# A graph network kernel: four accumulator banks in the adjacency stage, row groups released before the fourth scatter of the next, 125-row transfers in two parts

## The reference

```
row = concat(src, loops); col = concat(dst, loops)
deg = segment_sum(ones, col); dinv = rsqrt(deg); w = dinv[row] * dinv[col]
h = x
5 times: h = 0.2 * segment_sum(w * h[row], col) + 0.8 * x
x = layernorm(x + h)

gate = silu(edge_attr @ W1.T + b1) @ W2.T + b2 + sum(emb[z[src]] * (emb[z[dst]] @ adaptW.T))
cw   = where(dist < 6, 0.5 * (cos(pi * dist / 6) + 1), 0)
msg  = gate * x[dst] * cw * mult[dst]
agg  = segment_sum(msg, src) / segment_sum(mult[dst], src)
x = layernorm(x + layernorm_gamma_beta(x + agg))
```

## Time and profile before

| | us |
|---|---|
| median of 3 runs | 4159.2 |
| lowest and highest | 4145.71, 4161.85 |
| the profiled execution | 4189.48 |
| its span, first to last instruction | 4187.5 |
| mean granted TensorE clock in it | 0.763 |

### The profile page before, as it was taken

One profiled execution on the slowest core, in us unless ns is written; L12 is line 12 of the kernel. 1 busy time (PEld: TensorE's weight loads), 2 busy tenths in 40 slices (PEclk: granted clock), 3 DMA queues, 4 the chain that ended last, 5 costly groups with the idle time before them and its releaser, 6 DMA issues. The chain is left out here.

```text
span 4187.5 us, 105568 instructions
## 1 busy us (share of the span) xinstructions
PE 2724.7 (65%) x35364; PEld 2317.5 (55%) x35364; DVE 2724.8 (65%) x5976; ACT 1370.5 (33%) x4059; POOL 2366.0 (57%) x2008
## 2 busy tenths in 40 slices
PE   0455555555656457777877777877737777777773
PEld 0344343344434246667766766766737777677673
DVE  3876676677667454544554454554478888888887
ACT  0443333333334211111110111111136666666662
POOL 1266776777667635555555555655545555555552
PEclk9975555555555578888998888988968788888886
DMA  4543343333342277777878778877646666666663
GB/s 178 185 154 125 124 157 121 139 139 140 139 127 90 84 267 285 285 280 283 294 277 296 273 270 299 293 274 288 234 163 225 213 222 215 214 219 214 218 221 96
DMA packets 228041, 871.37 MB, mean 208 GB/s; under 512 B 89156, under 2 KB 148420, under 8 KB 182787
## 3 DMA queue, kind: packets, MB, share of 16 engines
q1 hardware_dynamic: 166914, 728.89, 48.8%
q10 hardware_dynamic: 9696, 96.89, 5.8%
q0 software_dynamic: 51232, 42.56, 3.4%
HBM read 670.80 MB, written 197.52 MB: 207 GB/s over the span
## 5 line engine op out<-in xcount | busy, mean ns | idle before, releaser
L705 POOL DMA_INDIRECT slot_table<-w_pay,w_slot x1568 | 1773.3, 1131 | 1166.2 <-PEq L1217 509.6
L1219 PE MATMUL pL<-p_parts,p_adj 128*128 128x144 bf16 x12250 | 978.9, 242 | 350.8 <-issue 241.3
L1219 PEld LDWEIGHTS pL<-p_parts,p_adj 128*128 128x128 bf16 x12250 | 891.5, 106 | 433.2 <-issue 429.3
L1031 PE MATMUL pA<-ohk,ohb 128*128 128x98 bf16 x3200 | 359.1, 275 | 550.3 <-ACT adj L1067 370.1
L1031 PEld LDWEIGHTS pA<-ohk,ohb 128*128 128x128 bf16 x3200 | 257.5, 131 | 680.8 <-ACT adj L1067 430.4
L1587 ACT ACTIVATE h_all<-c_rows,c_ac 128x48 f32<-128x48 f32 x2401 | 561.1, 323 | 66.6 <-DVE c_ac L1556 66.6
L1067 ACT ACTIVATE adj<-pA 128x392 bf16<-128x392 f32 x800 | 368.5, 494 | 539.5 <-remote 297.1
L1463 POOL TENSOR_TENSOR c_msg<-c_msg 128x637 f32<-128x637 f32 x196 | 232.8, 1188 | 481.1 <-DVE c_msg L1525 481.1
L792 ACT ACTIVATE w_hid<-w_pH,b1c 96x512 f32<-96x512 f32 x196 | 133.7, 682 | 919.7 <-PE w_pH L740 487.9
L1662 PE MATMUL cG<-c_tabp,c_ohT 128*128 128x81 bf16 x7056 | 369.6, 222 | 4.2 <-DVE c_msg L1525 2.6
L1662 PEld LDWEIGHTS cG<-c_tabp,c_ohT 128*128 128x128 bf16 x7056 | 346.1, 112 | 5.2 <-DVE c_msg L1525 3.1
(11 more groups left out here) (277 smaller groups left out, 3266.5 us busy)
## 6 DMA issues: line engine op xcount, KB each, us to landing
p_adj<-adj_table SPq DMA_DIRECT2D x250, 1568.0 KB
c_lanes<-lane_table SPq DMA_DIRECT2D x150, 768.0 KB, 6.7
adj_table<-adj ACTq DMA_DIRECT2D x50, 1568.0 KB
c_rows<-slot_table SPq DMA_DIRECT2D x255, 255.0 KB, 3.9
slot_table<-zero SPq DMA_DIRECT2D x42, 1249.5 KB
c_lanes<-lane_table SPq DMA_DIRECT2D x50, 832.0 KB
w_attr<-in_edge_attr_dram SPq DMA_DIRECT2D x49, 640.0 KB
slot_table<-w_pay,w_slot POOLq DMA_INDIRECT x1568
```

The lines of the kernel that those rows point to most:

```text
L705: pool.indirect_dma_start(slotT, bass.IndirectOffsetOnAxis(ap=slot[:, t:t + 1], axis=0), pay[:, t, :], None, bounds_check=SLOTS - 1, oob_i ...
L1031: m = nc.tensor.matmul(pA[:, n % 2, j * KG:(j + 1) * KG], ohb[:, b % OB, g * (PT // 2) + j, :], ohk[:, b % OB, g * (PT // 2) + j, :])
L1219: x_ = nc.tensor.matmul(pL[:, half, o * H3:(o + 1) * H3], adj[:, q, n * P:(n + 1) * P], parts[:, n, :, :].rearrange("p t f -> p (t f)"), s ...
```

## The change

Three edits.

Transfers of 124 or 125 rows are split at row 112 (`SPW`): the loads of `dst`, `src` and `ew`, the eight stores of `key_sb` and the store of `cw`. The counts that are waited for follow.

`pA` has four banks for two. PSUM has room for it because `pR` is gone: `labels` write into the unused end of bank 1 of `w_pG`, `offsets` into that of bank 0, and `pC` has a bank of its own in the index stage. In the adjacency stage the gates of chunk 0, which write bank 0, also wait until `off_b` has been copied; in the propagate stage the flag `offsets_first` is False and they don't.

In `scatter`, the wait for the landing of the chunk before and the count of `s_free` stand before the fourth scatter of a chunk, for after its eighth.

```
+    SPW = 112
...
-                pC, pZ, pQ = win.pR, win.pG, win.pT
+                pC = ps("pC", [P, 512], c=c)
+                pZ, pQ = win.pG, win.pT
...
-                            sp.dma_start(shifted[n, 0:E].rearrange("(p j) -> p j", p=SP_), key_sb[:, n * AL:n * AL + ST]).then_inc(s_edge, 16)
+                            to = shifted[n, 0:E].rearrange("(p j) -> p j", p=SP_)
+                            sp.dma_start(to[0:SPW, :], key_sb[0:SPW, n * AL:n * AL + ST]).then_inc(s_edge, 16)
+                            sp.dma_start(to[SPW:SP_, :], key_sb[SPW:SP_, n * AL:n * AL + ST]).then_inc(s_edge, 16)
...
-                        pool.wait_ge(s_edge, 16 * (SH + 1))
+                        pool.wait_ge(s_edge, 16 * (2 * SH + 1))
...
-            pR = ps("w_pR", [P, 512], c=c)
+            GATES = CT // 2 * 2 * H
+            assert GATES + P <= 512 and GATES + NB <= 512
+            offs = pG[:, 0, GATES:GATES + NB]
+            labs = pG[:, 1, GATES:GATES + P]
...
                     for t in range(a, b):
+                        if t == a + 3:
+                            v = (q - 1) % MC
+                            n = 16 * (chunks[v][1] - chunks[v][0])
+                            pool.wait_ge(s_sc[v], w * n + n)
+                            pool.sem_inc(s_free, 1)
                         if before_each:
                             before_each(t)
...
-                    v = (q - 1) % MC
-                    n = 16 * (chunks[v][1] - chunks[v][0])
-                    pool.wait_ge(s_sc[v], w * n + n)
-                    pool.sem_inc(s_free, 1)
...
-            def gates(pe, w, q):
+            def gates(pe, w, q, offsets_first):
...
+                if q == 0 and offsets_first:
+                    pe.wait_ge(s_offb, w + 1)
...
-                nc.tensor.matmul(pR[:, P:2 * P], ones_w[:, :], diag[:, :]).then_inc(s_lab, 1)
+                nc.tensor.matmul(labs, ones_w[:, :], diag[:, :]).then_inc(s_lab, 1)
...
-                nc.tensor.matmul(pR[:, 0:NB], before[:, :], tot[:, :]).then_inc(s_off, 1)
+                nc.tensor.matmul(offs, before[:, :], tot[:, :]).then_inc(s_off, 1)
...
-                nc.scalar.activation(off_b[:, :], pR[:, 0:NB], ACT.Copy).then_inc(s_offb, 1)
+                nc.scalar.activation(off_b[:, :], offs, ACT.Copy).then_inc(s_offb, 1)
...
-                pA = ps("pA", [P, 2, 512], c=c)
+                BANKS = 4
+                pA = ps("pA", [P, BANKS, 512], c=c)
...
-                                    m = nc.tensor.matmul(pA[:, n % 2, j * KG:(j + 1) * KG], ohb[:, b % OB, g * (PT // 2) + j, :],
+                                    m = nc.tensor.matmul(pA[:, n % BANKS, j * KG:(j + 1) * KG], ohb[:, b % OB, g * (PT // 2) + j, :],
...
-                        act.sem_inc(s_ev, 2)
+                        act.sem_inc(s_ev, BANKS)
...
-                                        act.dma_start(tile[0:SP_ - 1, :], bass.AP(table.tensor, 0, [[ST, SP_ - 1], [1, ST + HALO]])).then_inc(s, 16)
+                                        for a, b in ((0, SPW), (SPW, SP_ - 1)):
+                                            act.dma_start(tile[a:b, :], bass.AP(table.tensor, a * ST, [[ST, b - a], [1, ST + HALO]])).then_inc(s, 16)
...
-                                    act.dma_start(ew[:, :], edge_weight.rearrange("(p j) -> p j", p=SP_)).then_inc(s_edges[2], 16)
+                                    for a, b in ((0, SPW), (SPW, SP_)):
+                                        act.dma_start(ew[a:b, :], edge_weight.rearrange("(p j) -> p j", p=SP_)[a:b, :]).then_inc(s_edges[2], 16)
```

More of the change, by code:

```diff
@@ L62, in gnn @@
     SP_ = 125
+    SPW = 112
+    assert 0 < SPW < SP_ - 1
     ST = E // SP_
@@ L411, in zero_first @@
                         act.wait_ge(s_z, 1)
-                        act.wait_ge(s_edge, 16 * (SH + 1))
+                        act.wait_ge(s_edge, 16 * (2 * SH + 1))
                         for n in range(DG):
@@ L436, in _ @@
                             sp.dma_start(degT.rearrange("(c l d) -> l c d", l=P, d=GR), degp[:, :, :]).then_inc(s_degT, 16)
-                        sp.wait_ge(s_st, 16)
+                        sp.wait_ge(s_st, 32)
                     @block.gpsimd
@@ L498, in _ @@
                     def _(dve):
-                        dve.wait_ge(s_dst, 32)
-                        dve.wait_ge(s_src, 32)
+                        dve.wait_ge(s_dst, 48)
+                        dve.wait_ge(s_src, 48)
                         nc.vector.scalar_tensor_tensor(key_sb[:, :], dst_sb[:, :], 13, src_sb[:, :], ALU.logical_shift_left,
@@ L545, in _ @@
                         nc.vector.memset(zero[:, :], 0.0).then_inc(s_z, 1)
-                        dve.wait_ge(s_ew, 16)
+                        dve.wait_ge(s_ew, 32)
                         cut(dve)
@@ L750, in gates, with pe_parts @@
                 x_.then_inc(s_g, 1)
-            def pe_parts(pe, w, n):
+            def pe_parts(pe, w, n, offsets_first=True):
                 if 2 <= n < MC + 2:
-                    gates(pe, w, n - 2)
+                    gates(pe, w, n - 2, offsets_first)
                 if 1 <= n < MC + 1:
@@ L863, in counts @@
                 dve.wait_ge(s_lab, w + 1)
-                nc.vector.scalar_tensor_tensor(before[:, :], pR[:, P:2 * P], label[:, :], to_here[:, :], ALU.is_equal, ALU.mult)
+                nc.vector.scalar_tensor_tensor(before[:, :], labs, label[:, :], to_here[:, :], ALU.is_equal, ALU.mult)
                 step(nc.vector.tensor_tensor(firsts[:, :], carry[:, :], run[:, :, WT - 1], ALU.subtract))
@@ L902, in edge_windows @@
             win.labels, win.act_offsets = labels, act_offsets
-            win.pG, win.pR = pG, pR
+            win.pG = pG
             win.load_keys, win.load_attr = load_keys, load_attr
@@ L1225, in body @@
                                         if turn < win.turns:
-                                            win.pe_parts(pe, w, turn)
+                                            win.pe_parts(pe, w, turn, False)
                                     if v == 0 and piece == 3:
```

6 lines of the change are left out of this document (3 added, 3 removed).

## The result

The changed kernel takes 4101.7 us (median, 4096.3 to 4111.2), the kernel before 4158.5. The ratio is 0.9871, with an interval of 0.9844 to 0.9899: 57 us less. The forecast was 128 us less. The stated range held the time, but the likeliest case was not the one that came: rival C (4111) was nearer.

What follows compares the result with a forecast made beforehand. No engine over 65% busy; it blamed slow 125-row transfers in the front and TensorE and ScalarE in lockstep on two banks in the adjacency stage. 4189.5 - 48 - 80 - 30.3 gave 4031 us, range 3960 to 4120.

Steps and rivals of the forecast that it cites:

- the likeliest case: Whole kernel: front and banks gain as forecast, 4031 us, own range 3985 to 4085, chance 0.45.
- rival C: Adjacency stage: banks are not the cause, groups end late otherwise, stage stays at 1270.5; 4111 us, chance 0.25.
- Setup, -10.5: Front: split loads bring key_sb near 13.7 us, the last weight load then being late; -10.5 us, poor end -6.
- Edge stores, -38: Front: split key_sb stores at 413 GB/s hide VectorE's 38.66 us of idle time; -38 us (-30 to -38.7).
- The case of 300 GB/s: Edge stores at only 300 GB/s: first group at key_sb + 38.5, 2.6 us of VectorE's idle time stays.
- Front: Setup and edge stores together: -48 us (-36 to -49), 0 if splitting does nothing.
- Four banks, -80: Adjacency stage: TensorE runs ahead of ScalarE's evictions; -80 us, between 62 and 105, bounded by 152 of excess.
- Release, 0: Scatters of both stages: release before the fourth scatter, its new landing wait taken as costing 0 us.
- The bound of +113: Adjacency scatters: most the new landing wait could cost, 1.2 us for each of 96 groups.
- rival E: Adjacency scatters: landings run later than four pitches and each of 96 groups waits; slower, up to 4224 us, chance 0.05.
- Labels and offsets, 0: Adjacency gates: waiting also for off_b costs 0 us, 24 us as the poor end.
- The 30.3 us: Whole kernel: profiled execution, 4189.5 us, lies 30.3 us above the median of runs, 4159.2; taken off at the end.

Runs made afterwards that it cites:

- chip g: The chip of one group of follow-up runs, on which the kernel before takes 4157.5 us.
- chip f: The chip of another group of follow-up runs, on which the kernel before takes 4187.0 us.
- f_split: The kernel before with the row splits alone, where the kernel before takes 4187.0 us: ratio 0.9893.
- f_split_banks: The changed kernel with the release put back behind the eighth scatter, where the kernel before takes 4187.0 us: ratio 0.9975.
- e_after: The changed kernel itself, on the chip where the kernel before takes 3683.1 us: ratio 1.039.
- e_split: The kernel before with the row splits alone, where the kernel before takes 3683.1 us: ratio 0.9893.
- e_split_banks: The changed kernel with the release put back behind the eighth scatter, where the kernel before takes 3683.1 us: ratio 0.9883.
- g_half: The changed kernel with every second scatter left out in both stages, waits and counts kept: ratio 0.8329 to the kernel before.
- h_rows64: The changed kernel with every scatter kept but carrying 64 of its 128 rows: ratio 0.9897 to the kernel before.
- h_pace: The changed kernel with a GpSimd fill and a drain before each scatter: ratio 1.7134 to the kernel before, 7107 us.

## Why the prediction was right or wrong

**Setup, -10.5: -4.3.** What is late next was named rightly, the last weight load, but not its landing. It was issued at 8.73 and the transposes start at 16.97, 8 us later; the sum had 3.9, taken for the median landing of scatters (see below on rows 9). The poor end of -6 was not poor enough.

**Edge stores, -38: -31.8** between key_sb and VectorE's first group. The stores ran at 299 GB/s and a share of 0.90, not at 413 and 1.01, so they took 23.6 us where the sum had 18.0. The case of 300 GB/s stood in the text, with the group at key_sb + 38.5 and 2.6 us left; measured are key_sb + 42.8 and 6.78, since the gathers took 17.2 us to the first group for 12.6. VectorE was free when expected (55.89, key_sb + 36.0). The share of the engines decides, as the row of 0.32 for 125 rows said. The Trainium skill's page "DMA: Bandwidth & Descriptors" has two rules for it, and the runs divide them: splitting by rows is not useless here (the row on partition halves in "Rules for kernel authors" goes by a premise, that both parts use all 16 engines anyway, which 0.32 contradicts for 125 rows), and the number of engines that divides the row count ("Why a DMA increments its semaphore by 16 and not by 1") agrees with 0.32 before and 0.90 after. Front: -38.1 for -48 (4.3 + 31.8, and 2.0 in smaller waits up to the first scatter), within its bounds of -36 to -49.

**Four banks, -80: 0.** This is the step that failed. The stage is 1244.9 us with two banks and 1242.0 with four when the release is early (chip g), and 1262.2 and 1302.3 when it is late (chip f); on the chip with prompt counts 1164.0 and 1162.4. The sum took the 69% of TensorE's waits that ended with an eviction as time that banks would free. But the evictions were late because their counts were, and with more banks the same lateness showed elsewhere. From f_split to f_split_banks TensorE's waits for an eviction fall from 253.1 to 185.9 us, while its waits for the one-hots rise from 18.0 to 157.1 and VectorE's for `s_free` from 172.8 to 326.3. In the kernel after, GpSimd's turn waits did fall by 80 us, and its landings (37.5), its slower scatters (17) and TensorE's waits for the one-hots came instead. In a ring of four engines that wait for each other, the share of one edge is not the share of the gain. Rival C had the right row, the 4.48 us at 674.94, and its own mechanism is what was found; 0.25 was too little for a rival with a row against a forecast with a ratio. The low end of the forecast's own range is also miscounted: 152 x 0.69 with a good front gives 4005, not 3985.

**Release, 0: -51 us in the adjacency stage with four banks on chip f, no gain shown with two; +44 to +48 there and +121 to +126 in the propagate stage where counts are prompt.** The bound of +113 from landings of 6.3 us was the right mechanism (rival E), and was put out of the sum by a median of 3.9 that is not a landing of scatters at all. The view of the earlier trace rows takes in everything that touches `slot_table`, and the page of the kernel before shows which transfers have a landing:

```profile
c_rows<-slot_table SPq DMA_DIRECT2D x255, 255.0 KB, 3.9
...
slot_table<-w_pay,w_slot POOLq DMA_INDIRECT x1568
```

The 2.5/3.9/6.3 are those of SyncE's loads from the table in the convolve stage; the scatters have none. That 6.3 is close to their true landings is luck. By the completion counts of e_after, as read above, their medians are 6.0 to 6.2 us in the propagate stage, and by chunk 2.2 to 7.4 in the adjacency stage. The prediction also counted on GpSimd's 496.6 us of waits for TensorE as room in the propagate stage; they hold on the chips with late counts and are 107.2 us in e_split, where counts are prompt. E was to decide at a mean landing of 5.6 us; it decided by the chip.

**Labels and offsets, 0: near 0.** No run has them without anything else; e_split and e_split_banks, which differ by them and the banks, are 2 us apart, and in the kernel after TensorE's gates wait 8.6 us in all for `off_b`, in 3 waits.

**The 30.3 us** between the profiled run and the median were rightly taken off: the profile after shows no such excess. What they were is not shown.

## What to carry to other kernels

Before a gain is worked out from waits, ask whether the producer was late or only its count: an instruction that waits for its own engine's earlier count, with nothing else between, tells it, and buffers don't cure it. A transfer's landing has to be read for that transfer, in the stage where it will be waited for: a view by tile mixed in other transfers, and 3.9 us stood where the scatters have 6.0. A row without a landing, like that of the scatters, is a warning. And a wait that is free where an engine idles is not free when another chip lets it run: of the parts here the row split alone lowers the time on one chip of each kind, 0.989 on both, and is the one to keep everywhere (the changed kernel is 0.985 to 0.987 on one kind and 1.039 on the other).

## What the runs showed of the hardware

Transfers of 125 rows moved 133 GB/s with a share of 0.32; the same bytes as 112 and 13 rows 299 GB/s with 0.90 (before at 50 to 60 us, after at 22 to 42).

On three of four chips the counts of VectorE and TensorE reach their waiters late while scatters of GpSimd follow at 1.28 us, and on one chip they do not: by the measure of the table, e_split and e_after have no delay over 1 us. In the piece shown ScalarE waits 8.77 us and VectorE 6.71. It depends on the number of scatters, not on their rows (g_half, h_rows64). What carries the counts, and why the chips differ, stays open. The trace of a chip of the late kind also holds fewer of the scatters' completion records: 1546 to 3380 for each chunk's semaphore in the kernel before, 5977 to 6922 in e_split, where 392 scatters of 16 counts make 6272. (The semaphores take some other counts as well.) h_pace, on a chip of the late kind but without delays, has them all. Late counts and lost records go together; whether the recording has a part in the lateness is not shown. The cost is large: with half of the scatters left out the kernel took 0.833 of the time, and the one chip without it takes 3683 us for what the others do in 4147 to 4187.

Four accumulator banks for two left TensorE 620.3 us busy for 713.0 in the adjacency stage, at a mean granted clock of 0.62 for 0.52 (e_split_banks, e_split), with no gain in time.

A drain of GpSimd behind a fill, between two scatters, left 1.86 us of idle time each.
